# A feed-forward kernel's first block: x by 32x32 squares in two halves, W1 in four pieces on two queues, three folds of W1 ahead of the products, norms multiplied into x and not into W1

## The reference, cut to what matters

```
q_left_n  = q_left  / sqrt(sum(q_left**2)  + 1e-8)      # norms per lane
q_right_n = q_right / sqrt(sum(q_right**2) + 1e-8)
x_rot = hamilton(q_left_n, hamilton(x * gate, conj(q_right_n)))   # (tokens, 256)
probs = softmax(x_rot @ Wr.T)                            # 8 experts
h     = gelu(x_rot @ W1[7] + b1[7])                      # 256 -> 1024
out   = x + (h @ W2[7] + b2[7]) * probs[:, 7:8]          # 1024 -> 256
```

## Time and profile before

| | us |
|---|---|
| median of three runs | 107.02 |
| lowest, highest run | 105.79, 107.14 |
| the profiled execution's own time | 105.98 |
| its span in the trace | 104.2 |
| TensorE busy | 100.1 |
| DVE busy | 66.5 |
| ACT busy | 48.9 |
| POOL busy | 25.7 |

### The profile page before, as it was taken

The page is one execution under the profiler, slowest core; times in us unless marked ns, Lnnn a source line. Parts: engine busy times, 40 slices in busy tenths (PEclk is TensorE's granted clock), DMA queues, the critical chain, the costliest instruction groups (busy, mean ns, idle before and its releaser), DMA issues.

```text
span 104.2 us, 1505 instructions
## 1 busy us (share of the span) xinstructions
PE 100.1 (96%) x572; PEld 84.9 (82%) x572; DVE 66.5 (64%) x143; ACT 48.9 (47%) x79; POOL 25.7 (25%) x16
## 2 busy tenths in 40 slices
PE   7899999999999999999999999999999999999990
PEld 7679888878888888888888878788888878888980
DVE  1599589878264999288224997272494972378451
ACT  5046794444441484484424544834424544442700
POOL 3400000029999300000000000069998000000000
PEclk9999999999999999999999999999999999999998
DMA  1999910170004222350600050000006040000005
GB/s 25 287 388 369 178 26 6 42 159 0 0 0 123 88 101 101 74 127 0 200 2 3 0 208 0 0 0 0 0 0 201 6 201 0 0 0 0 0 5 196
DMA packets 9222, 8.12 MB, mean 78 GB/s; under 512 B 6784, under 2 KB 7424, under 8 KB 9216
## 3 DMA queue, kind: packets, MB, share of 16 engines
q1 hardware_dynamic: 8928, 7.78, 25.4%
q10 hardware_dynamic: 288, 0.26, 0.7%
HBM read 5.94 MB, written 2.10 MB: 77 GB/s over the span
## 4 chain that ended last, share of the span: by engine, by line
PE 91%; DMA 4%; SPq 1%; DVE 1%; DVEq 0%; issue 0%
PE pre L627 40%; PE acc L634 25%; PE acc L642 15%; DMA x_in<-in_x 4%; PE pre L597 3%; PE lT_bank L586 2%; PE acc L638 1%; PE acc L636 1%; DVE y L462 1%; PE extra L568 1%; PE acc L568 1%; PE lT_bank L568 1%; PE acc L696 1%; SPq L217 0%; SPq L214 0%; DVEq L69 0%
## 5 line engine op out<-in xcount | busy, mean ns | idle before, releaser
L304 ACT ACTIVATE h_hi<-pre,quats 128x512 fp32r<-128x512 f32 x32 | 22.1, 690 | 43.5 <-PE pre L627 42.5
L428 DVE TENSOR_TENSOR h_lo<-h_all,h_hi 128x512 fp32r<-128x512 f32 x32 | 21.8, 690 | 20.1 <-ACT h_all L308 19.8
L634 PE MATMUL acc<-w_parts,h_hi 128*128 128x512 f32 x116 | 32.3, 391 | 0.0
L634 PEld LDWEIGHTS acc<-w_parts,h_hi 128*128 128x128 f32 x116 | 21.5, 188 | 4.5
L627 PE MATMUL pre<-xT_hi,w_hi 128*128 128x512 f32 x60 | 24.0, 400 | 0.0
L627 PE MATMUL pre<-xT_lo,w_hi 128*128 128x512 f32 x60 | 23.7, 394 | 0.0
L642 PE MATMUL acc<-w_parts,h_lo 128*128 128x256 f32 x128 | 23.0, 283 | 0.0
L266 POOL TENSOR_TENSOR exps<-e_const,shifted 128x32 f32<-128x32 f32 x4 | 22.2, 5577 | 0.2
L642 PEld LDWEIGHTS acc<-w_parts,h_lo 128*128 128x128 f32 x128 | 20.0, 189 | 2.7 <-DVE h_lo L428 0.7
L308 ACT ACTIVATE h_all<-pre,quats 128x512 f32<-128x512 f32 x32 | 21.8, 683 | 0.0
L627 PE MATMUL pre<-xT_hi,w_lo 128*128 128x512 f32 x60 | 18.7, 392 | 0.0
(11 more groups left out here) (68 smaller groups left out, 59.3 us busy)
## 6 DMA issues: line engine op xcount, KB each, us to landing
x_sq<-in_x SPq DMA_DIRECT2D x12, 128.0 KB, 3.6
x_in<-in_x SPq DMA_DIRECT2D x3, 512.0 KB, 3.4
out<-y SPq DMA_DIRECT2D x3, 512.0 KB, 2.6
w<-in_W SPq DMA_DIRECT2D x4, 256.0 KB, 6.3
w_rest<-in_W_rest SPq DMA_DIRECT2D x1, 768.0 KB, 5.8
x_in<-in_x SPq DMA_DIRECT2D x2, 256.0 KB, 3.9
w_first<-in_W_first SPq DMA_DIRECT2D x1, 264.0 KB, 2.7
out<-y SPq DMA_DIRECT2D x2, 128.0 KB, 1.7
```

Source lines behind the costliest of these rows:

```text
L304: nc.scalar.activation(h_hi[:, s, :], pre[f % 2][:, :], ACT.Gelu, bias=b1_cols[:, f:f + 1]).then_inc(h_hi_ready, 1)
L428: nc.vector.tensor_tensor(h_lo[:, s, :], h_all[:, s, :], h_hi[:, s, :].bitcast(F32), ALU.subtract).then_inc(h_lo_ready, 1)
L634: nc.tensor.matmul(acc[j][:, :], rows, w2_parts[:, f, :, :], start=(f == 0), stop=False)
```

## The change

Block 0's x is loaded by squares too, in two halves of 256 contiguous tokens, each by four DMAs of 64 KB. DVE transposes each half (turn_first_x), ACT and DVE make the high and low parts, one k at a time. TensorE's transposes and ACT's copies are gone. W1_rest is laid out in three contiguous pieces of 256 KB, loaded separately: W1_first and the first piece from ACT's queue, the second behind half 0 and the third behind half 1 on SP's. The scale is multiplied into xT (ACT with a scale per partition, DVE with a scalar) and no longer into R or chunk 0; the router's weights still take it. Fold 0, 1 and 2 stand ahead of the opening, fold 3 behind it. ACT makes chunk 0's high part. The rows x_in of block 0, b2 and the squares of block 1 are loaded behind W2; block 0's output and x_in follow the order of tokens by halves. One more warm-up product.

```diff
-    WARM_UP = 6
+    WARM_UP = 7
...
+    HALF = BLOCK // 2
+    first_tokens = x[0, 0:BLOCK, :].rearrange("(h p j) c -> p h (j c)", h=2, p=P)
+    first_squares = x[0, 0:BLOCK, :].rearrange("(h t n) (q c) -> h q t n c", h=2, t=SQ, q=QUADS)
...
+        fold_banks = [None] + [bank[:, :].rearrange("p (k f) -> p k f", k=KC) for bank in (acc[3], lT_bank, extra)]
...
             sp.dma_start(quats[:, :], small).then_inc(q_loaded, 16)
-            sp.dma_start(w1_first[:, :, :], W1_first).then_inc(w1_loaded[0], 16)
-            for i in range(2):
-                tiles = slice(i * TT // 2, (i + 1) * TT // 2)
-                sp.dma_start(x_in[:, tiles, :], x_blocks[0, :, tiles, :]).then_inc(first_x_loaded[i], 16)
-            sp.dma_start(w1_rest[:, :, :], W1_rest).then_inc(w1_loaded[1], 16)
+            for half in range(2):
+                rows = slice(half * QUADS * TT // 2, (half + 1) * QUADS * TT // 2)
+                for q in range(QUADS):
+                    sp.dma_start(x_sq[q * SQ:(q + 1) * SQ, rows, :], first_squares[half, q]
+                                 ).then_inc(first_sq_loaded[half], 16)
+                sp.dma_start(w1_rest[:, half + 1, :, :], W1_rest[half + 1]).then_inc(w1_loaded[half + 2], 16)
             for i in range(FT // W2_TILES):
                 tiles = slice(i * W2_TILES, (i + 1) * W2_TILES)
                 sp.dma_start(w2[:, tiles, :], W2[i]).then_inc(w2_loaded[i], 16)
+            sp.dma_start(b2_all[:, :], b2.to_broadcast([P, C])).then_inc(b2_loaded, 16)
+            sp.dma_start(x_in[:, :, :].rearrange("p (h j) c -> p h (j c)", h=2), first_tokens).then_inc(x_loaded, 16)
 
             def load_squares(b):
                 for q in range(QUADS):
                     sp.dma_start(x_sq[q * SQ:(q + 1) * SQ, :, :], x_squares[b, q]).then_inc(x_sq_loaded, 16)
 
+            sp.wait_ge(x_turned, turned(0))
             load_squares(1)
...
             act.wait_ge(warm_zeroed, 1)
+            act.dma_start(w1_first[:, :, :], W1_first).then_inc(w1_loaded[0], 16)
+            act.dma_start(w1_rest[:, 0, :, :], W1_rest[0]).then_inc(w1_loaded[1], 16)
             nc.scalar.activation(gelu_scratch[:, :], warm[:, :], ACT.Gelu)
 
             def split_x(b, k):
 
-                act.wait_ge(x_turned, KC * (b - 1) + k + 1)
-                nc.scalar.activation(xT_hi[b % 2][:, k, :], xT[b % 2][:, k, :], ACT.Copy).then_inc(xT_hi_ready, 1)
+                act.wait_ge(x_turned, turned(b - 1) + k + 1)
+                nc.scalar.activation(xT_hi[b % 2][:, k, :], xT[b % 2][:, k, :], ACT.Copy,
+                                     scale=scale[:, k:k + 1]).then_inc(xT_hi_ready, 1)
...
             def split_first_x(half):
-                act.wait_ge(first_x_turned, half + 1)
-                nc.scalar.activation(xT_hi[0][:, :, half * HALF:(half + 1) * HALF], xT_ps[half],
-                                     ACT.Copy).then_inc(xT_hi_ready, 1)
+                for k in range(KC):
+                    act.wait_ge(x_turned, KC * half + k + 1)
+                    nc.scalar.activation(half_of(xT_hi[0][:, k, :], half), half_of(xT[0][:, k, :], half), ACT.Copy,
+                                         scale=scale[:, k:k + 1]).then_inc(first_xT_hi_ready, 1)
+
+            def first_w1_high(k):
+                act.wait_ge(folded, k + 1)
+                nc.scalar.activation(w1_hi[:, k, chunk(0)], first_fold_banks[k], ACT.Copy
+                                     ).then_inc(w1_first_hi_ready, 1)
...
-            for half in range(2):
-                split_first_x(half)
-            for half in range(2):
-                copy_first_x(half)
+            for k in range(KC):
+                first_w1_high(k)
+            split_w1(1)
+
+            act.wait_ge(scale_ready, 1)
+            split_first_x(0)
+            split_w1(2)
+            split_first_x(1)
             for b in range(N_BLOCKS):
                 for f in range(FT):
                     gelu(b, f)
                     if b == 0 and f == 0:
-                        split_w1(2)
                         split_w1(3)
...
+            def split_first_x(half):
                 for k in range(KC):
-                    mine = slice(4 * k, 4 * k + 4)
-                    nc.vector.tensor_scalar(R[:, mine, :], R_raw[:, mine, :], scale[:, k:k + 1], None,
-                                            ALU.mult).then_inc(R_ready, 1)
-
-            def split_x(b, k):
-                dve.wait_ge(xT_hi_ready, KC * b + k + 1)
-                nc.vector.tensor_tensor(xT_lo[b % 2][:, k, :], xT[b % 2][:, k, :],
-                                        xT_hi[b % 2][:, k, :].bitcast(F32), ALU.subtract).then_inc(xT_lo_ready, 1)
-
-            def split_first_x(half):
-                tokens = slice(half * HALF, (half + 1) * HALF)
-                dve.wait_ge(xT_hi_ready, half + 1)
-                nc.vector.tensor_tensor(xT_lo[0][:, :, tokens], xT_ps[half], xT_hi[0][:, :, tokens].bitcast(F32),
-                                        ALU.subtract).then_inc(xT_lo_ready, 1)
-
-            def first_w1_high(k):
-
-                dve.wait_ge(folded, k + 1)
-                nc.vector.tensor_scalar(w1_hi[:, k, chunk(0)], first_fold_banks[k], scale[:, k:k + 1], None,
-                                        ALU.mult).then_inc(w1_first_hi_ready, 1)
+                    dve.wait_ge(first_xT_hi_ready, KC * half + k + 1)
+                    nc.vector.scalar_tensor_tensor(
+                        out=half_of(xT_lo[0][:, k, :], half), in0=half_of(xT[0][:, k, :], half), scalar=scale[:, k:k + 1],
+                        in1=half_of(xT_hi[0][:, k, :], half).bitcast(F32), op0=ALU.mult,
+                        op1=ALU.subtract).then_inc(first_xT_lo_ready, 1)
+
+            def turn_first_x(half):
+                dve.wait_ge(first_sq_loaded[half], 16 * QUADS)
+                rows = slice(half * QUADS * TT // 2, (half + 1) * QUADS * TT // 2)
+                for k in range(KC):
+                    nc.vector.transpose(
+                        half_of(xT[0][:, k, :], half).rearrange("p (j t s) -> p j s t", j=TT // 2, s=QUADS),
+                        x_sq[:, rows, k::KC].rearrange("p (s j) c -> p j s c", j=TT // 2)
+                        ).then_inc(x_turned, 1)
 
             def first_w1_low(k):
                 dve.wait_ge(w1_first_hi_ready, k + 1)
...
             for k in range(KC):
-                first_w1_high(k)
-            for k in range(KC):
                 first_w1_low(k)
-            for half in range(2):
-                split_first_x(half)
-            scaled_rotation()
+            turn_first_x(0)
+            split_first_x(0)
+            turn_first_x(1)
+            split_w1(1)
+            split_first_x(1)
             dve.wait_ge(wr_padded, 1)
             for k in range(KC):
                 take_router(k)
             split_w2(0)
-            split_w1(1)
...
             def fold(i):
-                if i == 1:
-                    pe.wait_ge(w1_loaded[1], 16)
-                    pe.wait_ge(R_ready, KC)
-                elif i == 3:
-
-                    pe.wait_ge(xT_lo_ready, 2)
-                    pe.wait_ge(xT_copied, 2)
+                pe.wait_ge(w1_loaded[i], 16)
                 for k in range(KC):
-                    nc.tensor.matmul(fold_banks[i][:, k, :], R[:, 4 * k:4 * k + 4, :], w1_rest[:, k, chunk(i - 1)],
+                    nc.tensor.matmul(fold_banks[i][:, k, :], R[:, 4 * k:4 * k + 4, :], w1_rest[:, i - 1, k, :],
...
                 pe.wait_ge(w1_first_hi_ready, KC)
                 for half in range(2):
-                    pe.wait_ge(xT_hi_ready, half + 1)
+                    pe.wait_ge(first_xT_hi_ready, KC * (half + 1))
                     for f in range(2):
                         products(w1_hi, xT_hi, half, f)
                     if half == 0:
                         pe.wait_ge(w1_first_lo_ready, KC)
                     for f in range(2):
                         products(w1_lo, xT_hi, half, f)
-                for f in range(2):
-                    for half in range(2):
-                        pe.wait_ge(xT_lo_ready, half + 1)
-                        last = products(w1_hi, xT_lo, half, f, ends=True)
-                    last.then_inc(pre_done, 1)
+                    pe.wait_ge(first_xT_lo_ready, KC * (half + 1))
+                    for f in range(2):
+                        last = products(w1_hi, xT_lo, half, f, ends=(half == 1))
+                        if half == 1:
+                            last.then_inc(pre_done, 1)
...
-            pe.wait_ge(R_raw_ready, 1)
+            pe.wait_ge(R_ready, 1)
             first_fold()
-            pe.wait_ge(ident_ready, 1)
-            channels = x_in[:, :, :].rearrange("p j (m k) -> p j k m", k=KC)
-            for half in range(2):
-                pe.wait_ge(first_x_loaded[half], 16)
-                for k in range(KC):
-                    for j in range(TT // 2):
-                        last = nc.tensor.transpose(xT_ps[half][:, k, j * P:(j + 1) * P],
```

(38 more changed lines are left out.)

53 lines of the change are left out of this document (20 added, 33 removed).

## The result

The changed kernel took 107.66 us in the median of 20 runs (106.97 to 108.32), the kernel before 106.72 in the median of 20 (105.66 to 107.70): 0.94 us more. The profiled execution has a span of 105.8 us against 104.2, 1.6 more. It took 107.63 us, its kernel's median, but that of the kernel before took 105.98, well under its median, so the two traces lie further apart than the medians.

A forecast was written before the change was run, and what follows sets the result against it. The prediction took TensorE, busy 96% of the span, as the bound, so the change was worth what it moved tile 2's first product. It added 0.1 us there and 0.2 for fold 1's piece: 107.02 + 0.3 = 107.3 us, range 105.7 to 108.9.

The forecast's parts named there:

- My own sign of being wrong altogether: TensorE after tile 2: new gaps there, or a granted clock under 1, would show the prediction wrong altogether.
- Baseline, tile 2 at 12.68: Kernel before: tile 2's first product read from the chain of waits as 12.68 us; the change put it at 12.76, +0.1.
- I take 0.43: SP's queue, block 0's squares: each 64 KB issue takes 0.43 us, so half 1's last is issued at 5.0.
- the cover of half 1: Opening: half 1's squares land by 7.75 us, wanted at 8.38, with 0.5 to 0.6 us of cover.
- Fold 1's piece, +0.2: W1_rest's first piece on ACT's queue: wanted at 5.26 us, taken to land at 5.5, adding 0.2 us.
- The chain of DVE and ACT: Ahead of the opening: transposes, xT_hi and xT_lo in series; opening at 7.98, half 1 at 10.06, tile 2 at 12.76.
- Two more us cost nothing: Block 1's squares: landing by 17 us, turned at 16.8, needed by the router only at 20.95; cost nothing.
- Rival 2: SP's queue fills: half 1's issues take 1.28 us each, landing at 10.4, 2.0 late; 109.3 us, chance 0.20.
- Rival 3: DVE's transposes of block 0's halves cost 0.45 us each; 106.2 us, bound 105.5, chance 0.20.
- Rival 4: ACT loads its table (1.28 us) ahead of its two issues, fold 0 0.7 later; 108.0 us, chance 0.10.
- My 156 to 212 GB/s: Front loads: bounds on the rate of squares; at 200 half 0 lands at 5.8 us, at 156 half 1 at 8.4.
- the prediction's estimate of 280 GB/s: Front loads: squares at 8/11 of 387 GB/s; half 0 near 5.4 us, half 1 near 7.0, sum 0.1 not 0.3.

The follow-up runs named there:

- A2: The changed kernel run once more, unchanged, for a second profile: span 105.4 us, tile 2 1.27 us late against the kernel before.
- E5: Changed kernel with b2 and x_in issued behind block 1's squares and all three W1_rest pieces from ACT's queue: ratio 1.0239 to the kernel before.
- E2: Changed kernel with all three pieces of W1_rest issued from ACT's queue, leaving SP's two issues out: ratio 1.0213 to the kernel before.
- E7: Changed kernel with block 0's half 0 by rows through TensorE, half 1 by squares, folds and late loads reordered: ratio 0.9974 to the kernel before.
- E10: E7 with an eighth warm-up product: ratio 0.9927 to the kernel before, median 106.01 us against E7's 106.36.

## Why the prediction was wrong, step by step

I forecast 107.3 us, +0.3, as the likeliest, with 0.84 for a change within 2%. The time lay in the range, the change within 2%, and the sign was that of my small term; but the kernel is slower by 0.94 us in the medians and 1.5 by the ratio, three to five times what I gave and clear of the noise. That 107.3 comes so near to 107.66 is luck: I started from a median of three runs, 107.02, which lay 0.3 above that of the 20. My own sign of being wrong altogether, a new gap behind tile 2, is in the trace, at the router.

- **Baseline, tile 2 at 12.68.** Wrong reading, 0.3 us: it starts at 12.36.
- **"I take 0.43" for a 64 KB issue.** This is the step that failed in both executions of the changed kernel, and it made the cover of half 1 vanish. It took 0.61 (the other bound, 0.57, was nearly right). Half 1's last issue began at 6.38 and not at 5.0, half 1 was turned from 8.78 and not 8.38, its products began at 10.46 and not 10.06: 0.4 us. DVE was ready for it earlier than I had thought, at 8.08, and stood 0.69 for the DMA where I had a cover of 0.6. In A2 it was worse, products at 10.80. I took the value by the number of runs (256); the row that was nearest in kind, 32 partitions of 256 B runs, was the other one.
- **Fold 1's piece, +0.2.** Wrong the other way. It landed 3.2 us behind its issue at 1.31, at 4.5, and fold 1 began at 4.96. It was the second piece that came late: issued at 3.82 and in at 6.7, where TensorE was free for it at about 6.0. Its fold started at 6.81, and the opening began right behind it at 7.71. I had given it cover until 7.1, and it used nearly all of it.
- **The chain of DVE and ACT.** Sizes right within 0.1: pairs of transposes 1.09, pairs of xT_hi 0.91 to 0.97, xT_lo 0.89. The opening at 7.71 against 7.98, as fold 0 started 0.15 earlier and its first record took 0.54 and not 0.70. From half 1's start (10.46) to tile 2 (13.37) it took 2.91, against 2.70 in my sum: half of the rest lies between h_all's end (13.22) and the product, 0.15 where I had 0.03.
- **"Two more us cost nothing" for block 1's squares.** The cover was right, the landing wrong: by 17 in my sum, 20.17 measured. SP's last W2 issue began at 9.1, b2 and x_in went first, and the second issue of squares took 1.83, but the last one, from 13.68, ended at 14.85, within my "end by 15". It then took 5.3 us to land where I had 2, with b2's and x_in's 0.64 MB still under way: x_in, issued at 10.04, needed 8.2. Price: 0.50 at the router and 0.16 behind it in this trace, none in A2; I had put this term at nothing.
- **Rival 2** had the right mechanism, half 1 landing behind 8.4, but I priced it by a queue that fills (1.28 an issue). Until 7 us no issue took over 0.66; each was simply slow. **Rival 3** did not occur: transposes of 256 columns took 0.60 to 0.64, not 0.45. **Rival 4** did not either: ACT's issues came first, at 0.90.

For the pair of traces the terms add up: my 0.3, 0.3 for the baseline, 0.4 for half 1, 0.2 from half 1 to tile 2, 0.66 at and behind the router, less the 0.2 of fold 1's piece, come to 1.7, and the spans differ by 1.6.

What held half 1 back was the issue and not the bytes, by these rows. The last issue of its squares, at 6.38, landed 2.4 us later, the shortest of the eight. In the changed kernel all DMA together moved 104 GB/s from 7 to 8 us with half of the engines' time unused (that stretch of the changed kernel, columns as in E5's table); 64 KB in 0.61 us are 107 GB/s:

```profile
7.00:8.00 1.00, 1.00 (x6) 0.81 (x6) 0.82 (x3) 0.59 (x3) 0.00 (x0) 1.00 0.46 104
```

My 156 to 212 GB/s came from block 2's squares, and these too are near what SP's queue gave out: four issues of 128 KB in 2.58 us, from 18.85 on, are 203 GB/s. The DMA engines' busy share was 0.58, 0.68 and 0.96 in the three microseconds from 20 to 23. The last, in the kernel before:

```profile
22.00:23.00 1.00, 1.00 (x8) 0.82 (x5) 0.86 (x3) 0.00 (x0) 0.12 (x1) 1.00 0.96 212
```

A row of 128 KB issues thus says about twice too much for 64 KB issues, which take as long each. So my rate did not decide half 1's landing; by these rows it was the issuing queue, but no run took the issues away and left the bytes and their shape.

The Trainium skill (DMA: Bandwidth & Descriptors, section "Why small descriptors are slow") counts 11 cycles where 8 carry data for 256 B, which gave the prediction's estimate of 280 GB/s. The row above is lower, 212 GB/s with the engines nearly always busy, and half 1's landing did not hang on either figure.

## What to carry to other kernels

Cost a DMA at the head of a kernel by its issue as well as by its bytes, from a row of the same shape: a load cut in eight costs its queue eight times, and everything behind it in that queue. Moving large loads to a second queue need not relieve small ones on the first: in E2 it made them at least 2.3 us late. When a change takes work from the busiest engine and puts two engines in series ahead of it, try half of it: one half by the old way can cover the new way's latency for the other, as in E7 and E10. And before two traces are compared, set the time of each beside the median of its kernel.

## What the hardware showed that I had not expected

- The issue of 64 KB in 256 runs of 256 B to 32 partitions took 0.57 to 0.66 us on SP in the changed kernel, that of 128 KB in 512 such runs 0.63 in the median and 1.83 at the most. That of 256 KB in 128 runs of 2 KB took 0.43 for W2, but 0.60 for W1's pieces that stand right behind squares.
- TensorE's first products run at half pace up to a moment that differs between executions of one kernel: fold 0 of the kernel before took 1.37 us in one trace and 2.10 in another, and the spans were 104.2 and 106.2 us. The granted clock reads 1.00 (2.4 GHz) in that stretch of the slower one. What sets the moment stays open.
- After a wait of 2.9 us the granted clock fell to 0.50 (1.2 GHz) in E5's trace, and stayed there for 3 us; after the waits of 1.1 and 2.06 us in the traces of the changed kernel and E2 it read 1.00.
